# Two attention-and-experts layers on one core: rows asked for ahead of weights, key products of layer two moved, unread products before two waits

## The chip, the cores and the metric

The kernel runs on one core of a Trainium2 chip. The metric is the device time of one launch in microseconds. The engines are TensorE (PE), VectorE (DVE), ScalarE (ACT), GpSimd (POOL) and SyncE (SP), which issues most of the DMAs. They run side by side and wait for each other by semaphores.

## The reference

Four residual steps on `x` of 4 batches x 1024 tokens x 256 values, all in float32:

```python
x = x + attn0(norm(x), ctx, mask)   # 8 heads of 64, 64 context rows of 192 per batch, masked softmax
x = x + ffn0(norm(x))               # 8 experts, top 1, at most 640 rows each: relu(t @ W1) @ W2, W1 256x1024
x = x + attn1(norm(x), ctx)         # 16 heads of 64, no mask
x = x + ffn1(norm(x))               # 8 experts, top 2: silu(t @ W11) * (t @ W12) @ W2, W11 and W12 256x512
```

An expert's rows are picked by the data. In the last step each token goes to its two best experts, and the two results are weighted and added.

## The kernel before, in words

**Attention.** Each layer folds the keys into the query weights and the values into the output weights (`m` and `n`), so that a tile of 128 tokens needs scores (L666), a softmax (ACT L731, POOL L763), a transpose of the probabilities (L638) and the product with `n` (L681). 32 tiles run in a software pipeline: iteration `t` of every engine's list works on tile `t` and, ahead of it or behind it, on others. NT is 32. Every product is made of three matmuls on numbers split in a high part (made by ACT) and a low part (made by DVE): transposed probabilities are split by ACT L712 and DVE L971 before L681 may start. The router's logits (L687) and ranks (L696, L698, L700) are TensorE's too; DVE works out the routing (L806 to L858) in a long row of small steps, one of which (L825) reads exponentials that ACT makes (L725). POOL then scatters each tile's normed rows to their expert in HBM (L752).

**Keys of layer two.** The keys and values of layer two need only the context and weights. They are 16 units (`tensor_kv`, L342), each of two products on 256 columns (four records in the profile), and each is copied out of PSUM by ACT (L350). `KV_AT` gives the units that stand in iterations of layer one's attention, `KV_AFTER` the rest, which come after it. Within an iteration they stand at the end, after the logits; ACT's copies of the same units stand before its softmax and before L725.

**First experts.** SP waits until all scattered rows have landed (`rows_landed`, twelve semaphores), asks for expert 0's rows (`E_xin`, 640 KB), then stores the keys. TensorE finishes `KV_AFTER`, transposes the rows (L1125), ACT and DVE split them (L1192, L1237), and then come 96 matmuls up (L1144) and 120 down (L1161) for each of 8 experts. ACT splits the down weights (L1185) between the last key copy and the rows.

**Second experts.** The routed rows stand in 39 tiles of 256 rows, two tiles in flight (`par`). For tile `i` TensorE makes 48 matmuls up (L1433), four transposes of tile `i+1` (L1406) and 24 matmuls down for tile `i-1` (L1418). A tile's rows (`E_xin`, 260 KB) come with 4 values each, from which DVE makes the row's weight and its place in the output in six small steps (`meta`, `NM` = 6, L1503 to L1508): one after each of four products `E_hf` (L1522), and the last two at the end of the tile (`small.more(NM)`). SP's loop asks for tile `i+1`: the up weights (L1366, 2048 KB), the rows (L1381), the down weights (L1374, 512 KB). A table in SBUF says of each tile whether its expert differs from that two tiles before; where it does not, the weight DMAs are issued but move nothing. The up weights wait until the up products of tile `i-1` are done. The rows wait for all six `meta` steps and for the transposes of tile `i-1`. SP works in order, so what stands behind a waiting instruction waits too. Before each weight DMA SP loads two values from the table.

Of the kernel before, what the change touches and what calls it, by code (L numbers as in the profile page):

```python
# [15 lines left out]
P = 128  # L16
B, SEQ, D = 4, 1024, 256
TOK = B * SEQ
NT = TOK // P
# [21 lines left out]
def is_int(v):  # L41
    return isinstance(v, (int, np.integer))
# [160 lines left out]


ZEROED = 16 * (2 * E + 2)
VECTOR = 2 * E + 1


def attention_setup(p, layer, ins, base, before):
# [3 lines left out]
    PR, W, INNER = H // 2, H * KEYS, H * DH  # L213
# [41 lines left out]
    N_BANK, RING_N = 4, 3  # L255
    UNITS = 2 * PR // 4
    KV_BANKS = (0, 1, 2, 3)
    KV_AT = {NT: range(0, 2), NT + 1: range(2, 5)}
    KV_AFTER = range(5, 2 * PR)

    def kv_ps(j):
        return ps[:, KV_BANKS[j % len(KV_BANKS)], 0:B * KEYS]
# [196 lines left out]
def attention(p, layer, ins, setup, base, before):  # L459
# [8 lines left out]
    PR, W = H // 2, H * KEYS  # L468
# [84 lines left out]
    def cnt(t):  # L553

        return max(0, min(t + 1, NT))
# [64 lines left out]
    def tensor(e, ahead=None):  # L620
        e.wait_ge(p.s_sel, 3)
        for t in iters:
# [33 lines left out]
            if ok(t + 3):  # L656
# [3 lines left out]
                for q in range(NB):  # L660
                    bank = ps[:, S_BANK + ((t + 3) % 2) * NB + q, :]
# [6 lines left out]
                                          stop=(c == KC - 1 and j == 2))  # L668
                mm.then_inc(s_sim, 1)

            need(e, s_res, cnt(t - 1))
            need(e, s_lg, cnt(t - 3))
            if rank_at(t - 1) is not None:
# [10 lines left out]
            if ok(t - 2):  # L684
# [1 line left out]
                for c in range(KC):  # L686
                    mm = e.matmul(ps[:, O_BANK, LOGITS], xfT[:, c, :], wr[:, c, :], start=(c == 0), stop=(c == KC - 1))  # L687
                mm.then_inc(s_lgp, 1)
            if ahead and t in ahead.KV_AT:
                ahead.tensor_kv(e, ahead.KV_AT[t])  # L690
            g = rank_at(t)
            if g is not None:
# [332 lines left out]
def experts_capacity(p, ins, setup, rows_from):  # L1025
# [94 lines left out]
    def transposes(q, e):  # L1120
        q.wait_ge(s_x, 16 * (e + 1))
        wait(q, s_hlo, 2 * FC * e)
        for c in range(TC):
            for kc in range(KC):
                mm = q.transpose(ps[:, X_BANK + c, kc * P:(kc + 1) * P],  # L1125
                                 xin[:, c, kc * P:(kc + 1) * P], p.ident[:, :])
            mm.then_inc(s_xT, 1)

    def tensor(q):
        transposes(q, 0)  # L1130

        def up(e, par, h):
# [169 lines left out]
def experts_top2(p, ins, rows_from):  # L1302
# [3 lines left out]
    NM = 6  # L1306
# [46 lines left out]
    def sync(q):  # L1353
# [7 lines left out]
        def load_up(i, par):  # L1361
            e = expert(i)
            new = None if is_int(i) and i < 2 else changed(i)
            wait(q, s_up, FC * (i - 1))
            land(q, i)
            q.dma_start(up_w[:, par, :, :, :, :].rearrange("p j w c f -> p (j w c f)").bitcast(F32),  # L1366
                        up_d[e, :, :], cond=new).then_inc(s_w[par], 16)
# [24 lines left out]

        def body(i, par, last):
            if not last and not (is_int(i) and i == 0):
                load_up(i + 1, 1 - par)
                load_x(i + 1, 1 - par)
                load_w2(i + 1, 1 - par)
        tiles_loop(q, body)

    def tensor(q):  # L1400
# [41 lines left out]
                down(i, par)  # L1442
        rows_from.need(q, rows_from.s_lg, NT)
        rows_from.need(q, rows_from.s_posr, rows_from.GROUPS)
        transposes(0, 0)
        tiles_loop(q, body)

# [32 lines left out]
    def vector(q):  # L1480
# [36 lines left out]
        def body(i, par, last):  # L1517
            small = meta(i, par)
            for m in range(FC):
                q.wait_ge(s_sg, i * FC + m + 1)  # L1520
                wait(q, s_hlo, (i - 1) * FC + m + 1)
                q.tensor_tensor(hf[:, m, :], ps[:, UP_BANK + m, T1:2 * T1], sg[:, m, :],  # L1522
                                ALU.mult).then_inc(s_hf, 1)
                small.more(1)
                if m == 1:
                    split_w2(i, par)
                if 0 < m < 3:
                    hidden_lo(i, par, m - 1)
            if not last:
                split_x(i + 1, 1 - par)  # L1530
            for m in (2, 3):
                hidden_lo(i, par, m)
            small.more(NM)
            assert small.j == NM
            if not is_int(i) or i > 0:
                outputs(i - 1, 1 - par)
            wait(q, s_mt, NM * (i + 1))
            wait(q, s_add, 16 * TC * (i - 1))
            q.tensor_copy(dest[:, par, :, :], mb[:, :, :])
            if last:  # L1540
                outputs(i, par)
# [122 lines left out]
```

## Time and profile before

| | us |
|---|---|
| median of three timed runs | 1144.49 |
| their lowest and highest | 1144.35, 1146.0 |
| the profiled execution | 1133.49 |
| its span | 1131.7 |

The profiled execution lies 11.0 us under the median of the timed runs. Its time is 1.8 us more than its span. In the profile TensorE is busy for 92% of the span. Layer one's attention ends at about 191 us, the first experts run from 218 to 453, layer two's attention ends at about 746, and the second experts run from 762 to the end. The digits in the row of TensorE's clock are tenths of 2.4 GHz.

### The profile page before, as it was taken

How to read it: one execution, taken by the hardware profiler on the slowest of the kernel's cores; microseconds unless marked ns; L12 is line 12 of the kernel's file. 1: busy time of each engine (PE TensorE's matmuls, PEld its weight loads, DVE VectorE, ACT ScalarE, POOL GpSimd, SP SyncE). 2: the span in 40 equal slices, each digit the busy share in tenths (PEclk: the TensorE clock that was granted, in tenths of full speed). 3: DMA queues.
4: the chain of work that ended last, by engine and by line, in shares of the span. 5: the costliest groups of instructions: out<-in, count | busy, mean ns of one | idle time of the engine just before them, and what ended most of it. 6: DMA issues, size and time to landing. Idle time of an engine off the chain costs nothing.

```text
span 1131.7 us, 25652 instructions
## 1 busy us (share of the span) xinstructions
PE 1044.6 (92%) x7860; PEld 974.0 (86%) x7860; DVE 733.8 (65%) x2273; ACT 672.3 (59%) x2491; POOL 518.5 (46%) x527
## 2 busy tenths in 40 slices
PE   6999997899999999889999999719999999999994
PEld 4688886799999999569999999609999999999994
DVE  6678886344444443867787777646666777766673
ACT  2788885444444443579999999504444444444441
POOL 1346777333333332336588886751333333333333
PEclk9999999799999999999999999958999999999998
DMA  9910002556666657201122221453757755498432
GB/s 323 338 53 25 29 30 80 210 192 226 223 229 229 224 186 234 75 14 39 39 72 71 73 75 57 161 187 117 229 110 201 242 145 158 95 340 252 104 63 29
DMA packets 91045, 163.53 MB, mean 144 GB/s; under 512 B 11858, under 2 KB 70100, under 8 KB 88532
## 3 DMA queue, kind: packets, MB, share of 16 engines
q1 hardware_dynamic: 72868, 134.07, 34.5%
q0 software_dynamic: 17376, 27.15, 11.4%
q10 hardware_dynamic: 720, 1.33, 0.3%
q8 instruction: 39, 0.64, 0.2%
q14 instruction: 42, 0.34, 0.1%
HBM read 159.46 MB, written 63.34 MB: 197 GB/s over the span
## 4 chain that ended last, share of the span: by engine, by line
PE 79%; DVE 8%; DMA 5%; ACT 4%; issue 2%; POOL 1%; SPq 0%; DVEq 0%; ACTq 0%; POOLq 0%
PE psum L1433 15%; PE psum L681 11%; PE psum L666 11%; PE psum L1144 10%; PE psum L1161 10%; PE psum L1418 7%; DMA E_xin<-rows 4%; PE psum L638 4%; PE psum L342 2%; ACT L_prob L731 2%; PE psum L687 2%; PE psum L1406 2%; PE psum L379 1%; DVE L_m_lo L431 1%; PE psum L653 1%
## 5 line engine op out<-in xcount | busy, mean ns | idle before, releaser
L1552 POOL DMA_INDIRECT out<-E_y,E_dest x78 | 121.1, 1553 | 248.0 <-DVE E_y L1514 226.7
L731 ACT ACTIVATE L_prob<-psum,L_neg_max 128x64 f32<-128x64 f32 x768 | 228.6, 362 | 4.8 <-DVE L_neg_max L964 4.7
L1433 PE MATMUL psum<-E_xT_hi,E_up_w 128*128 128x256 f32 x1248 | 225.0, 280 | 2.9 <-DVE E_xT_lo L1493 2.9
L1433 PEld LDWEIGHTS psum<-E_xT_hi,E_up_w 128*128 128x128 f32 x1248 | 194.3, 190 | 3.5 <-DVE E_xT_lo L1493 3.5
L731 ACT ACTIVATION_READ_ACCUMULATOR L_prob<-psum,L_neg_max 128x1 f32 x768 | 195.4, 256 | 0.0
L1433 PE MATMUL psum<-E_xT_lo,E_up_w 128*128 128x256 f32 x624 | 174.6, 280 | 0.0
L1468 ACT ACTIVATE E_sg<-psum 128x256 f32<-128x256 f32 x156 | 59.9, 384 | 172.2 <-PE psum L1433 169.1
L1522 DVE TENSOR_TENSOR E_hf<-psum,E_sg 128x256 f32<-128x256 f32 x156 | 66.0, 423 | 91.6 <-ACT E_sg L1468 91.0
L1433 PEld LDWEIGHTS psum<-E_xT_lo,E_up_w 128*128 128x128 f32 x624 | 118.6, 190 | 0.0
L681 PE MATMUL psum<-L_n_hi,L_pT_hi 128*128 128x256 f32 x384 | 107.9, 281 | 10.9 <-DVE L_pT_lo L971 10.9
L763 POOL TENSOR_TENSOR L_prob<-L_prob,L_rcp 128x512 f32<-128x512 f32 (+1 forms) x64 | 94.3, 1474 | 41.0 <-DVE L_rcp L930 39.5
L1202 ACT ACTIVATE E_h_hi<-psum 128x256 fp32r<-128x256 f32 (+1 forms) x128 | 55.8, 437 | 89.2 <-PE psum L1144 89.2
L681 PE MATMUL psum<-L_n_hi,L_pT_lo 128*128 128x256 f32 x384 | 107.3, 279 | 0.0
L681 PE MATMUL psum<-L_n_lo,L_pT_hi 128*128 128x256 f32 x384 | 107.3, 279 | 0.0
L1245 DVE SCALAR_TENSOR_TENSOR E_h_lo<-psum,E_h_hi 128x256 fp32r<-128x256 f32 (+1 forms) x128 | 62.8, 491 | 55.4 <-ACT E_h_hi L1202 54.6
L1418 PE MATMUL psum<-E_w_hi,E_h_hi 128*128 128x256 f32 x312 | 90.2, 289 | 0.0
L1161 PE MATMUL psum<-E_w_hi,E_h_hi 128*128 128x256 f32 x320 | 90.2, 282 | 0.0
L1161 PE MATMUL psum<-E_w_hi,E_h_lo 128*128 128x256 f32 x320 | 89.6, 280 | 0.0
L1161 PE MATMUL psum<-E_w_lo,E_h_hi 128*128 128x256 f32 x320 | 89.5, 280 | 0.0
L1418 PE MATMUL psum<-E_w_hi,E_h_lo 128*128 128x256 f32 x312 | 87.0, 279 | 0.0
L1418 PE MATMUL psum<-E_w_lo,E_h_hi 128*128 128x256 f32 x312 | 86.9, 279 | 0.0
L681 PEld LDWEIGHTS psum<-L_n_hi,L_pT_hi 128*128 128x128 f32 x384 | 72.9, 190 | 14.9 <-issue 12.3
(198 smaller groups left out, 3089.8 us busy)
## 6 DMA issues: line engine op xcount, KB each, us to landing
E_up_w<-up SPq DMA_DIRECT2D x39, 2048.0 KB
E_w<-in_w SPq DMA_DIRECT2D x39, 512.0 KB
E_w<-in_w SPq DMA_DIRECT2D x16, 1024.0 KB, 7.3
E_xin<-rows SPq DMA_DIRECT2D x39, 260.0 KB, 2.7
E_raw<-in_w SPq DMA_DIRECT2D x16, 512.0 KB, 6.9
up<-E_raw_hi SPq DMA_DIRECT2D x16, 512.0 KB, 6.1
up<-E_raw_lo SPq DMA_DIRECT2D x16, 512.0 KB, 3.7
rows<-zero SPq DMA_DIRECT2D x8, 640.0 KB, 14.5
```

What stands on the lines that cost most here:

```text
L666: mm = e.matmul(bank, a[:, (t + 3) % 2, c, :], m[:, b, c, q * 512:(q + 1) * 512], start=(layer == 1 and c == 0 and j == 0), stop=(c == KC ...
L681: mm = e.matmul(o, a[:, r, :], m[:, b, r, :], start=(r == 0 and j == 0), stop=(r == PR - 1 and j == 2))
L731: last = e.activation(prob[q][:, h * KEYS:(h + 1) * KEYS], scores_ps(t)[:, h * KEYS:(h + 1) * KEYS], ACT.Exp, bias=nmx[:, q, h, :], accum_ ...
L763: e.tensor_tensor(pr, pr, rc[:, q, :, :].to_broadcast([P, H, KEYS]), ALU.mult).then_inc(s_p, 1)
L1144: mm = q.matmul(bank, a[par][:, c, m * P:(m + 1) * P], x[:, c, c0 * P:(c0 + cn) * P], start=(k == 0), stop=(k == 3 * KC - 1))
L1161: mm = q.matmul(bank, a[:, h, m, c * P:(c + 1) * P], w[par][:, m, :], start=(k == 0), stop=(k == 3 * FC - 1))
L1245: q.scalar_tensor_tensor(h_lo[:, h, m, 0:cn * P], ps[:, UP_BANK + m % 4, 0:cn * P], 0.0, h_hi[:, h, m, 0:cn * P].bitcast(F32), ALU.max, AL ...
L1418: mm = q.matmul(ps[:, Y_BANK + c, 0:D], a[:, par, m, c * P:(c + 1) * P], w[:, par, m, :], start=(k == 0), stop=(k == 3 * FC - 1))
L1433: mm = q.matmul(bank, up_w[:, par, half, w, c, m * P:(m + 1) * P], x[:, c, :], start=(k == 0), stop=(k == 3 * KC - 1))
L1468: q.activation(sg[:, m, :], ps[:, UP_BANK + m, 0:T1], ACT.Silu).then_inc(s_sg, 1)
L1522: q.tensor_tensor(hf[:, m, :], ps[:, UP_BANK + m, T1:2 * T1], sg[:, m, :], ALU.mult).then_inc(s_hf, 1)
L1552: q.indirect_dma_start(p.out[:, :], bass.IndirectOffsetOnAxis(ap=dest[:, par, c, :], axis=0), y[:, par, c, :], None, compute_op=ALU.add).t ...
```

## The change

Five edits. (1) In the second experts' SP loop the rows of tile `i+1` are asked for before its up weights. (2) DVE makes two `meta` steps after each of the first three `E_hf`, and none at the tile's end. (3) Six key units move into iterations NT-2 and NT-1, ahead of that iteration's wait for the split probabilities; two stand in NT and one in NT+1 (before: two and three), and seven after the attention (before: eleven). (4) and (5): before the transposes of the first experts and of the second experts TensorE waits for `rows_landed` and then makes six products of the identity with itself that nobody reads.

```diff
+def keep_busy(q, p, bank):
+    for j in range(6):
+        q.matmul(p.psum[:, bank, 0:P], p.ident[:, :], p.ident[:, :], start=True, stop=True)
...
-    KV_AT = {NT: range(0, 2), NT + 1: range(2, 5)}
-    KV_AFTER = range(5, 2 * PR)
+    KV_AT = {NT - 2: range(0, 3), NT - 1: range(3, 6), NT: range(6, 8), NT + 1: range(8, 9)}
+    KV_AFTER = range(9, 2 * PR)
...
+            if ahead and t < NT and t in ahead.KV_AT:
+                ahead.tensor_kv(e, ahead.KV_AT[t])
             need(e, s_res, cnt(t - 1))
...
-            if ahead and t in ahead.KV_AT:
+            if ahead and t >= NT and t in ahead.KV_AT:
                 ahead.tensor_kv(e, ahead.KV_AT[t])
...
     def tensor(q):
+        rows_from.rows_landed(q)
+        keep_busy(q, p, 5)
         transposes(q, 0)
...
             if not last and not (is_int(i) and i == 0):
+                load_x(i + 1, 1 - par)
                 load_up(i + 1, 1 - par)
-                load_x(i + 1, 1 - par)
                 load_w2(i + 1, 1 - par)
...
         rows_from.need(q, rows_from.s_posr, rows_from.GROUPS)
+        rows_from.rows_landed(q)
+        keep_busy(q, p, Y_BANK)
         transposes(0, 0)
...
-                small.more(1)
+                small.more(NM // 3)
...
-            small.more(NM)
             assert small.j == NM
```

TensorE's list in layer one's attention, iteration NT-2, before: the logits of the iteration before it (`wr`), the transposes of the probabilities (`L_prob_70`) and of the normed rows (`L_stage`), and the first product with `n`:

```order
L687 MATMUL psum<-wr,L_xfT 128x8 x2
L638 MATMUL psum<-ident,L_prob_70 128x128 x4
L653 MATMUL psum<-ident,L_stage 128x128 x2
L681 MATMUL psum<-L_n_hi,L_pT_hi 128x256
L681 MATMUL psum<-L_n_hi,L_pT_lo 128x256
L681 MATMUL psum<-L_n_lo,L_pT_hi 128x256
```

The same place now (lines are numbered anew by the change: L645, L660 and L690 are the old L638, L653 and L681, L349 the old L342):

```order
L696 MATMUL psum<-wr,L_xfT 128x8 x2
L645 MATMUL psum<-ident,L_prob_70 128x128 x4
L660 MATMUL psum<-ident,L_stage 128x128 x2
L349 MATMUL psum<-L_ctxT,L_wk 128x256 x6
L690 MATMUL psum<-L_n_hi,L_pT_hi 128x256
L690 MATMUL psum<-L_n_hi,L_pT_lo 128x256
L690 MATMUL psum<-L_n_lo,L_pT_hi 128x256
```

Six products, two for each of three key units, stand ahead of the product with `n`; iteration NT-1 has the same.

SP's list in the second half of the second experts' loop, before. `E_up_w` are the up weights, `E_xin` the rows, `tab` the table:

```order
L1359 TENSOR_LOAD tab
L1359 ISA x2
L1366 ISA
L1366 DMA E_up_w<-up 128x4096
L1377 ISA
L1377 TENSOR_LOAD tab
L1377 ISA x2
L47 REGISTER_ALU
L1381 ISA
L1381 DMA E_xin<-rows 128x2x260
```

The same place now (L1388 and L1392 are the old L1377 and L1381, L1366, L1370 and L1377 the old L1355, L1359 and L1366):

```order
L1388 ISA x2
L47 REGISTER_ALU
L1392 ISA
L1392 DMA E_xin<-rows 128x2x260
L1366 ISA
L1366 TENSOR_LOAD tab
L1366 ISA x2
L1370 ISA
L1370 TENSOR_LOAD tab
L1370 ISA x2
L1377 ISA
L1377 DMA E_up_w<-up 128x4096
```

Both table loads of the up weights (L1366, L1370) now stand between the DMA of the rows and that of the weights; before, they stood ahead of the weights' wait.

DVE's list in the same loop, before, from a tile's last `E_hf` on; `E_xT_lo` is the next tile's split, `E_mb` the last `meta` steps:

```order
L1522 TENSOR_TENSOR E_hf<-psum,E_sg 128x256
L47 REGISTER_ALU
L1506 SCALAR_TENSOR_TENSOR E_mb<-E_xin,shift 128x2
L1493 TENSOR_TENSOR E_xT_lo<-psum,E_xT_hi 128x512
L1483 TENSOR_TENSOR E_h_lo<-E_hf,E_h_hi 128x256 x2
L47 REGISTER_ALU
L1507 TENSOR_TENSOR E_mb<-E_mb,spare 128x2
L47 REGISTER_ALU
L1508 TENSOR_TENSOR E_mb<-E_mb,E_xin 128x2
```

And now, from the tile's third `E_hf` on (L1535, L1506, L1496, L1520, L1521 are the old L1522, L1493, L1483, L1507, L1508):

```order
L1535 TENSOR_TENSOR E_hf<-psum,E_sg 128x256
L47 REGISTER_ALU
L1520 TENSOR_TENSOR E_mb<-E_mb,spare 128x2
L47 REGISTER_ALU
L1521 TENSOR_TENSOR E_mb<-E_mb,E_xin 128x2
L1496 TENSOR_TENSOR E_h_lo<-E_hf,E_h_hi 128x256
L1533 REGISTER_ALU
L1535 TENSOR_TENSOR E_hf<-psum,E_sg 128x256
L1506 TENSOR_TENSOR E_xT_lo<-psum,E_xT_hi 128x512
L1496 TENSOR_TENSOR E_h_lo<-E_hf,E_h_hi 128x256 x2
```

The last two `meta` steps stood behind the last `E_hf`, the split and two `E_h_lo`; now they stand ahead of all of them.

## Rows read from the trace of the kernel before

**Rows 1.** The page: busy time, TensorE's and the clock's tenths in 40 slices.
```profile
PE 1044.6 (92%) x7860; PEld 974.0 (86%) x7860; DVE 733.8 (65%) x2273; ACT 672.3 (59%) x2491; POOL 518.5 (46%) x527
PEclk9999999799999999999999999958999999999998
```

**Rows 2.** Chain of waits, second experts, longest pieces: start us, us, what.
```profile
881.81 6.76 DMA E_xin<-rows
...
888.61 0.66 PE psum L1406 x4
...
892.01 5.44 PE psum L1433 x48
897.45 0.44 PE psum L1406 x4
```

**Rows 3.** Waits from 730 to 1131 us: engine line <- releaser: us, times, longest.
```profile
PE psum L1406 <- DMA E_xin<-rows: 21.7, 8, 15.9
PEld psum L1406 <- DMA E_xin<-rows: 7.4, 8, 1.4
```

**Rows 4.** Timeline of SP, second experts: start us, us, what.
```profile
879.17 0.36 SPq L1366 DMA_DIRECT2D E_up_w<-up  x1
881.81 0.38 SPq L1381 DMA_DIRECT2D E_xin<-rows  x1
883.67 0.37 SPq L1374 DMA_DIRECT2D E_w<-in_w  x1
...
986.11 0.35 SPq L1366 DMA_DIRECT2D E_up_w<-up  x1
```

**Rows 5.** Timeline of DVE, 872 to 893 us: start us, us, what.
```profile
878.62 0.42 DVE L1522 TENSOR_TENSOR E_hf<-psum,E_sg 128x256 f32<-128x256 f32 x1
...
881.39 0.16 DVE L1508 TENSOR_TENSOR E_mb<-E_mb,E_xin 128x2 f32<-128x2 f32 x1
```

**Rows 6.** Windows: us, busy PE, PEld, DVE, ACT, POOL, PEclk, DMA share, GB/s.
```profile
880.00:886.00 6.00, 6.00 (x55) 6.00 (x54) 3.87 (x13) 2.52 (x6) 2.84 (x2) 1.00 0.96 353
987.00:1024.00 37.00, 35.06 (x303) 34.42 (x302) 24.85 (x75) 16.78 (x40) 12.44 (x8) 1.00 1.02 337
```

**Rows 7.** Timeline of PE, 172 to 222 us: with idle before and its releaser.
```profile
184.38 0.36 PE L681 MATMUL psum<-L_n_hi,L_pT_hi 128*128 128x256 f32 x1 [1.29 <-DVE L_pT_lo L971]
...
218.37 0.69 PE L1144 MATMUL psum<-E_xT_hi,E_w_hi 128*128 128x384 f32 x1 [2.54 <-DVE E_xT_lo L1237]
```

**Rows 8.** Timeline of ACT, 176 to 222 us.
```profile
210.63 0.38 ACT L350 ACTIVATE L_kv<-psum 128x256 f32<-128x256 f32 x1 [0.48 <-PE psum L342]
...
214.36 1.90 ACT L1185 ACTIVATE E_w_hi<-E_w 128x2048 fp32r<-128x2048 f32 x1
216.17 1.47 ACT L1192 ACTIVATE E_xT_hi<-psum 128x256 fp32r<-128x256 f32 x5
```

**Rows 9.** Timeline of DVE, 185 to 222 us.
```profile
201.72 0.17 DVE L825 TENSOR_REDUCE L_r<-L_ex 128x2 f32<-128x16 f32 x1 [2.61 <-ACT L_ex L725]
216.57 1.75 DVE L1237 TENSOR_TENSOR E_xT_lo<-psum,E_xT_hi 128x256 fp32r<-128x256 f32 x5 [5.34 <-ACT E_xT_hi L1192]
```

**Rows 10.** Line L1074 on SP, 200 to 215 us: issue, and us to landing.
```profile
L1074 SPq DMA_DIRECT2D E_xin<-rows x1: 367/367/367, 208.7 to 208.7; - x1
DMA to landing us min/median/max: 5.1/5.1/5.1
```

**Rows 11.** Windows around the two starts of the experts, columns as in Rows 6.
```profile
217.60:224.40 6.80, 6.03 (x19) 6.03 (x20) 1.83 (x5) 1.02 (x3) 3.30 (x1) 0.50 0.86 290
764.30:770.60 6.30, 6.21 (x29) 6.21 (x30) 0.79 (x4) 2.56 (x5) 0.00 (x0) 0.50 0.79 309
```

**Rows 12.** Chain of waits, start of the second experts.
```profile
758.92 2.77 DMA E_xin<-rows
...
761.83 1.10 PE psum L1406 x4
...
764.39 8.71 PE psum L1433 x48
```

## The prediction

> **What bounds the kernel now.** I read the page first: TensorE is busy for 92% of the span and its clock is at full level but for a dip where the second experts start [rows 1]. So time is to be had only where TensorE idles or runs at the lower clock. Next the chain of waits, which shows TensorE almost everywhere and, in the second experts, pieces of 6 to 7 us of "DMA E_xin<-rows" in seven places, of which one is shown [rows 2]. Such a piece is not its price: the transfer runs beside TensorE's work. The price is in the waits. TensorE waited 21.7 us for these rows, 15.9 of them before the first tile, so 5.8 us in seven places. Its weight loads give 7.4 us in eight places, none over 1.4 [rows 3]. The first transposes after such a wait also take 0.66 us where others take 0.44 [rows 2], and 5.8 + 7 x 0.22 = 7.3 us. I take 7.4 us as what the seven waits cost, about 1.06 each.
>
> Why the rows are late stands in SP's timeline. The up weights (2048 KB) are asked for at 879.17, the rows at 881.81, and the rows land 6.76 us after that [rows 2, 4]. SP sat between the two for `meta`, whose last step started at 881.39 [rows 5]. From 880 to 886 us the DMA engines moved 353 GB/s x 6.00 = 2118 KB [rows 6], about the weights (2048 KB are 2097 thousand bytes), and only after that the rows came.
>
> **The change: rows ahead of weights, and `meta` earlier.** The third `E_hf` started at 878.62 [rows 5]. One chained step more stands before it now, some 0.2 us, it takes 0.3 until the next may start, and two steps of 0.2 follow, so the last starts near 879.35 and not at 881.39. SP's DMA stood 0.42 behind it (881.39 to 881.81), so the rows are asked for near 879.8, with no 2 MB ahead of them. TensorE wants them at 888.61 less the wait of up to 1.4, at 887.2. That is 7.4 us for a transfer of 260 KB that took 2.77 us alone [rows 12]. All seven waits go, -7.4 us.
>
> What is late next are the up weights. They now stand behind the rows' wait, the rows' DMA and their own two table loads. From the rows' DMA to the down weights', with two table loads between, SP took 883.67 - 881.81 = 1.86 us [rows 4]. So the up weights are asked for at 879.8 + 1.86 = 881.7, 2.5 us later than before. If their bytes take as long (879.17 to 886.0 is 6.8 us), they land at 888.5. The up products would start at 892.01 - 1.4 = 890.6. The margin is 2.1 us, and no wait follows. The down weights are asked for 1.86 us later still, at 883.5, where they were (883.67). The tightest place is where four sets of weights follow each other. An issue of up weights that moves bytes takes about 0.36 us on SP, one that moves none 0.08; of the first kind the loop has fourteen, and four of them start tile after tile from 986.11 on [rows 4]. From 987 to 1024 us the DMA engines are full without a break (share 1.02) [rows 6], four sets in 37 us or 9.25 each, against a tile's pitch of 897.45 - 888.61 = 8.8. Each set falls back by 0.4 to 0.5, the fourth by about 2, which uses up the margin. I count 0.6 us lost there. DVE does the same steps, three of them earlier, beside waits for ACT. The second experts give -7.4 + 0.6 = **-6.8 us**. Bounds: -7.4, and above nothing if the weights come later than I reckon (a rival below).
>
> **Key units.** A unit takes 0.86 us at the full clock (0.48 + 0.38 between the starts of two copies) [rows 8]. In NT-2 and NT-1 TensorE idled 1.29 us before the product with `n`, waiting for DVE's split [rows 7]; three units take 2.6, so each of the two iterations is longer by 1.3 and the attention's end comes 2.6 us later. That is paid back in NT+1, where one unit stands for three: before, DVE sat 2.61 us at L825, whose exponentials ACT made only after its key copies [rows 9]. Now that wait goes. DVE's last routing steps, POOL's last scatters and SP's DMA for the first expert's rows (208.7 us) stay within 0.3 us of where they were. They land 5.1 us after it [rows 10], at 213.8.
>
> What moves is TensorE and ACT between the two. After the attention seven units stand and not eleven. The seventh copy started at 210.63 [rows 8], so ACT's split of the down weights (1.90 us from 214.36) now ends near 212.9, before the rows land, where it held up ACT's split of the rows until 216.17 [rows 8]. Now: rows at 213.8, the first pair of transposes 0.25, ACT's first of five pieces 0.3 (1.47 / 5) [rows 8], DVE's five 1.75 [rows 9], and the up products start near 216.2. With the clock at its lower level the ten transposes take 10 x 0.27 (four took 1.10 us at that level [rows 12]), and the start is 213.8 + 2.7 + 0.3 + 0.35 = 217.2. Before: 218.37 [rows 7]. The gain is 2.2 or 1.2; since TensorE now idles about 2 us before the rows, I take **-1.5 us**. Bounds: the clock's lower level lasted 6.8 us from there [rows 11], at a loss of half of it, 3.4 us. A phase of the clock that falls otherwise moves this by up to 1.7 either way, so from +0.5 to -3.5.
>
> **Unread products.** No row shows a float32 product of 128 columns that isn't a transpose. By the unit of keys (two products of 256 columns in 0.86 us) six take 1.3 us at full clock, 2.6 at half. Before the second experts they start no later than SP's DMA behind the same waits, 758.92, and end by 761.5, before the rows are in at 761.69 [rows 12]: hidden, with up to 0.4 us lost if a semaphore comes late. Before the first experts they run from about 211 to 213. Do they raise the clock? Before the second experts, TensorE was 6.21 of 6.30 us busy at 0.50, and before that the first up products 6.03 of 6.80 [rows 11]. A burst of 2.6 us and one of 1.1, with gaps of at least 0.3 and of 1.5, is less than what failed to raise it for 6 us there. I take 0, with bounds +0.4 and -7.3 (next part).
>
> **Sum.** -6.8 - 1.5 + 0 = -8.3 us. The profiled execution has 1133.49 (span 1131.7, 1.8 around it) and would have 1125.2. The timed runs' median is 1144.49, 11.0 above it, in a way that the profile doesn't show. I take the same difference for it: 1136.2.
>
> **Rivals.** (A) The clock rises early. The products that start at 764.39 took 8.71 us, a later tile's 5.44 [rows 2, 12], and the transposes 1.10 for 0.44: 3.9 us. With the 3.4 of the first experts 7.3 us more go: 1128.9. For it: only the lower level stands there. Against it: rows 11. Chance 0.10. The Trainium skill, "TensorE: Matmul & The Clock Gate", section "Part 1: The HAM clock gate", says that the throttled state is the default and that activity releases it; by that rule these unread products would bring such a gain, and the trace agrees only as far as work without gaps goes.
>
> (B) The keys bring nothing. If DVE's 2.61 us do not come back (another wait takes its place, as ACT's copies in NT-1 do to its exponentials), the rows land 2.6 us later, the first up products start near 218.9, and 0.5 us is lost instead of 1.5 won: 1138.2. For it: DVE's steps follow one upon another there. Chance 0.17.
>
> (C) The 11 us between timed and profiled execution are slower transfers. Then more than 7.4 us go with the waits. With half of the 11 in these places: 1130.7. Nothing in the profile shows it. Chance 0.08.
>
> (D) The change doesn't do what it says: the rows stay late in the sets that follow upon each other, since the previous down weights stand ahead of them in the queue. Then the three waits of that stretch and the weights' own lateness leave half of the 7.4: 1139.9. Against it: these are only 512 KB. Chance 0.05.
>
> (E) Slower: the up weights are late. They are asked for 2.5 us later in each of fourteen loads that move bytes. From ask to need there are 890.6 - 881.7 = 8.9 us. Once a load takes longer, each further 0.1 us costs up to 1.4 us in all, and from 9.5 us (14 x 0.6 = 8.4) the change loses. At 9.9 us it costs 14.0 for the 0.6 counted: -8.3 - 0.6 + 14.0 = +5.1, 1149.6. For it: a set in full traffic takes 9.25 us. Against it: that holds the down weights and the scattered results too, and the up weights come first but for the rows. Chance 0.08.
>
> **How the numbers follow.** The forecast has 0.52; its own range is 1134 to 1138.5. The range 1130.5 to 1141 holds it with B, C and D, and leaves out A and E, 0.18. About 0.2% (2.3 us) is what the measurement tells from no change. Faster: the forecast, A, B, C and most of D, less a small rest for sums that fail together: 0.85. Same 0.07, slower 0.08.
>
> **What would show it.** In the profile after: no wait of TensorE for `E_xin` behind the first tile; SP's DMA of the rows near 0.4 us behind the last `meta` step, that of the up weights 1.9 behind it; no wait of L1433's line for a DMA, except up to 0.6 us in the stretch of four sets. The attention of layer one ends 2.6 us later and the scatters don't. The first up products start at 216 to 217.4. The second experts' first 48 products take 8.7 us still. I am wrong if TensorE waits for `E_up_w` in more than two tiles, if the rows' DMA before the first experts moves by over 1 us, or if the clock row is higher at either start.

## The result, and the profile after

| | forecast | measured |
|---|---|---|
| median of the timed runs, us | 1136.2 (1130.5 to 1141) | **1127.0** (1123.5 to 1132.3, six runs) |
| the kernel before, beside it | | 1143.3 (1137.7 to 1146.0, six runs) |
| ratio to before | 0.993 | 0.9865, interval 0.983 to 0.9901 |
| profiled execution and span | 1125.2 | 1130.32, 1128.6 |

The change is faster, as forecast, but by 15.4 us (1143.3 x 0.0135) instead of 8.3, and the time lies below the range. In this document two kinds of number have to be kept apart. The two profiled executions lie only 3.2 us apart (1133.49 and 1130.32), the medians of the timed runs 16.3 us. So the gain must not be read from these two profiles alone.

The page after, the rows that answer to [rows 1]:

```profile
PE 1052.6 (93%) x7884; PEld 981.6 (87%) x7884; DVE 736.1 (65%) x2273; ACT 675.2 (60%) x2491; POOL 523.5 (46%) x527
PEclk9999999899999999889999999868999999999997
```

TensorE is busy 8 us longer, for the same products and twelve unread ones, of which 1.60 and 2.90 us are seen in its timeline. The rest goes with its clock: at the lower level a product takes longer, the clock's row has five slices of 8 where it had two, and the mean granted clock of the span is 0.964 where it was 0.972.

The steps of the second experts, against [rows 3 to 5]. DVE's third `E_hf` with the last `meta` steps behind it, then SP (start us, us, what), then TensorE's waits from 785 us on (us, times, longest), then TensorE's timeline of the same tile:

```profile
879.34 0.42 DVE L1535 TENSOR_TENSOR E_hf<-psum,E_sg 128x256 f32<-128x256 f32 x1
879.67 0.15 DVE L1520 TENSOR_TENSOR E_mb<-E_mb,spare 128x2 f32<-128x2 f32 x1
879.86 0.16 DVE L1521 TENSOR_TENSOR E_mb<-E_mb,E_xin 128x2 f32<-128x2 f32 x1
```

```profile
880.28 0.38 SPq L1392 DMA_DIRECT2D E_xin<-rows  x1
882.36 0.36 SPq L1377 DMA_DIRECT2D E_up_w<-up  x1
```

```profile
PE psum L1444 <- DMA E_up_w<-up: 1.0, 3, 0.4
```

```profile
879.11 0.60 PE L1417 MATMUL psum<-ident,E_xin 128*128 128x128 f32 x4
...
887.73 0.60 PE L1417 MATMUL psum<-ident,E_xin 128*128 128x128 f32 x4
891.43 0.38 PE L1444 MATMUL psum<-E_xT_hi,E_up_w 128*128 128x256 f32 x1 [0.36 <-DMA E_up_w<-up]
```

The rows are asked for 0.42 us behind the last `meta` step, and no wait for `E_xin` is left (the transposes of 887.73 have no idle time in brackets). Now the weights come last, in three tiles, for 1.0 us in all. The chain of waits has the piece that the forecast had reckoned with 6.8 us (an estimate from bytes; no row of the trace before has the landing of the weights):

```profile
882.36 8.95 DMA E_up_w<-up
```

The start of the first experts, against [rows 7, 8]: the chain of waits, and TensorE's timeline.

```profile
208.12 2.37 DMA rows<-L_stage,row
...
218.65 15.80 PE psum L1155 x96
```

```profile
213.33 1.60 PE L211 MATMUL psum<-ident 128*128 128x128 f32 x12 [0.47 <-ACT L_kv L357]
215.96 1.31 PE L1134 MATMUL psum<-ident,E_xin 128*128 128x128 f32 x10 [1.02 <-DMA E_xin<-rows]
```

The twelve records of L211 are the six unread products. The ten transposes behind them take 1.31 us, so the clock is at its full level there. Two windows tell of the clock (columns as in [rows 6]):

```profile
218.60:222.10 3.50, 3.45 (x11) 3.45 (x12) 0.56 (x1) 0.49 (x1) 1.09 (x1) 0.51 1.00 413
```

```profile
762.50:768.80 6.30, 4.02 (x17) 3.36 (x17) 0.69 (x1) 1.44 (x2) 0.00 (x0) 0.50 0.88 279
```

At the first start half level (0.51, which is 1.2 GHz) lasted 3.4 us, where it was 6.8 before [rows 11]. At the second start it went on, in spite of the six unread products, until 771.6 us.

All three signs that the prediction named for being wrong are there: TensorE waits for `E_up_w` in three tiles and not in two at most, SP asks for the first experts' rows at 210.82 us and not at 208.7, and the clock's row has an 8 at the first start where it had a 7. The experiments tell which of them matter.

### The profile page after: what moved, and what is told of

Same layout as the page of the kernel before. It is cut to its first block, busy times and chain, and to the rows that moved or that the text cites. A ratio compares the mean times of both kernels' runs of the same rounds, so it can differ in the third digit from the quotient of the medians.

```text
span 1128.6 us, 25710 instructions
## 1 busy us (share of the span) xinstructions
PE 1052.6 (93%) x7884; PEld 981.6 (87%) x7884; DVE 736.1 (65%) x2273; ACT 675.2 (60%) x2491; POOL 523.5 (46%) x527
## 4 chain that ended last, share of the span: by engine, by line
PE 81%; DVE 6%; DMA 4%; issue 3%; ACT 3%; POOL 1%; SPq 1%; DVEq 0%; ACTq 0%; POOLq 0%
PE psum L1444 17%; PE psum L690 12%; PE psum L673 11%; PE psum L1155 10%; PE psum L1172 10%; PE psum L1429 8%; PE psum L645 3%; DMA E_up_w<-up 2%; PE psum L386 2%; ACT L_prob L740 2%; PE psum L696 2%; PE psum L1417 1%; PE psum L660 1%; DVE L_m_lo L438 1%; PE psum L349 1%
## 5 line engine op out<-in xcount | busy, mean ns | idle before, releaser
L1564 POOL DMA_INDIRECT out<-E_y,E_dest x78 | 126.2, 1618 | 234.8 <-DVE E_y L1527 110.8
L690 PE MATMUL psum<-L_n_hi,L_pT_hi 128*128 128x256 f32 x384 | 109.0, 284 | 8.3 <-DVE L_pT_lo L980 8.3
L690 PE MATMUL psum<-L_n_lo,L_pT_hi 128*128 128x256 f32 x384 | 108.1, 282 | 0.0
L690 PE MATMUL psum<-L_n_hi,L_pT_lo 128*128 128x256 f32 x384 | 108.1, 282 | 0.0
L1535 DVE TENSOR_TENSOR E_hf<-psum,E_sg 128x256 f32<-128x256 f32 x156 | 65.7, 421 | 55.7 <-ACT E_sg L1481 54.9
L673 PE MATMUL psum<-L_m_hi,L_xT_hi 128*128 128x512 f32 x192 | 82.9, 432 | 2.0 <-ACT L_prob L740 2.0
```

What stands on the lines that cost most here:

```text
L673: mm = e.matmul(bank, a[:, (t + 3) % 2, c, :], m[:, b, c, q * 512:(q + 1) * 512], start=(layer == 1 and c == 0 and j == 0), stop=(c == KC ...
L690: mm = e.matmul(o, a[:, r, :], m[:, b, r, :], start=(r == 0 and j == 0), stop=(r == PR - 1 and j == 2))
L1564: q.indirect_dma_start(p.out[:, :], bass.IndirectOffsetOnAxis(ap=dest[:, par, c, :], axis=0), y[:, par, c, :], None, compute_op=ALU.add).t ...
```

## The experiments

"Ratio" is to the kernel before on the same chip, with its 95% interval. "Start to end" is from the second experts' first up product to the end of the span. It needs a profile and leaves out what happened earlier. Of each kernel I also read where the clock went to half level around the first experts' start. Most kernels here have one profile, so differences between profiles alone can be chance; the timed runs decide.

**How far the profile of before stands for the kernel.** No edit.

> The kernel before, unchanged, once more. Its profiled execution (span 1131.7 us) lay 10 us under its timed runs, and the change gained 15.4 us in the timed medians but only 3.1 us between the two profiles. Theory N (noise of the clock): what differs from execution to execution is where TensorE's clock falls to its lower level in the two attentions, and the second experts take 367 us from the first up product to the end in every execution of this kernel. Then this profile shows that stretch within 1.5 us of 367.3, and the rest longer by what the row of the granted clock shows. Theory T (transfers): the waits for E_xin in the second experts are longer in the slower executions. Then the stretch is 375 to 380 us and TensorE waits for E_xin 12 to 18 us there, not 5.8. Timed: within 0.3% of before in both.

Ratio 1.0007 (0.9981 to 1.0032), median 1142.35 of 12 runs (1136.7 to 1149.1), span 1138.8. The same kernel took 7.1 us longer in its second profile. Stage by stage from the span's start: 0.7 at the end of the first experts, 2.9 in attention two, 1.6 between SP's first ask for rows and the second experts' first up product (5.5 and 7.1 us), 1.9 from there to the end (367.3 and 369.2). TensorE's waits for the rows behind the first tile were not 5.8 us but:

```profile
PE psum L1406 <- DMA E_xin<-rows: 6.8, 9, 1.7
```

In attention two the two profiles differ in the stretches of 3 to 7 us at half clock: before had none between 489 and 508 us, this one has two, 494.8 to 498.2 and 505.0 to 508.4. The timed runs say the same: over the 32 of the kernel before on this chip, time and mean granted clock have a correlation of -0.77, and their mean clock is 0.965, where the profiled execution of before had 0.972. So the 11 us between profile and median were in the main a short profile with a high clock. For slower transfers (rival C) there is 1.0 us of waits in 7.1: it has nearly nothing to stand on.

**The parts alone, and the whole once more.**

```diff
# rows_first: edits 1 and 2
+                load_x(i + 1, 1 - par)
                 load_up(i + 1, 1 - par)
-                load_x(i + 1, 1 - par)
...
-                small.more(1)
+                small.more(NM // 3)
...
-            small.more(NM)
# keys_moved: edit 3
+    KV_AT = {NT - 2: range(0, 3), NT - 1: range(3, 6), NT: range(6, 8), NT + 1: range(8, 9)}
+    KV_AFTER = range(9, 2 * PR)
...
# unread: edits 4 and 5
+        rows_from.rows_landed(q)
+        keep_busy(q, p, 5)
...
+        rows_from.rows_landed(q)
+        keep_busy(q, p, Y_BANK)
```

> Edits 1 and 2 alone (rows asked for ahead of the up weights, two meta steps after each of the first three products); keys and unread products as before. Theory N: the second experts give the 7.5 us that lie between the two profiles there (367.3 against 359.8), so -7 us (0.994) and the other half of the 15.4 us comes from the other edits. Theory T: -12 to -16 us (0.987 to 0.990), nearly the whole.

> Edit 3 alone (six key units into NT-2 and NT-1, seven after the attention). By the prediction -1.5 us at most; by the profile after, where the first up products started at 218.65 us against 218.37, nothing. Theory N: the clock falls less often at the end of layer one's attention when TensorE is given work in NT-2 and NT-1, and -3 to -6 us come of it in the mean. Theory T: 0 to -1.5 us.

> Edits 4 and 5 alone (six unread products before the transposes of the first and of the second experts). The prediction: nothing. Theory N allows a part here: if the burst makes the clock rise one step earlier in a share of the executions, -1 to -3 us in the mean. Theory T: within 1 us.

> The changed kernel once more, on the same chip as the next three. So far: 0.9865 for it, and 0.9931, 0.9984 and 0.9975 for its parts alone, product 0.9890. Theory P (the parts add up): 0.988 to 0.990, -12 to -13 us. Theory I (keys and unread products help each other, or the rows first need one of them): 0.985 to 0.987, -15 to -17 us. The stretch from the first up product of the second experts to the end is 360 to 365 us, against 367 to 373 in kernels that ask for weights first.

| kernel | ratio | median, us | start to end, us |
|---|---|---|---|
| rows_first | 0.9931 (0.9907 to 0.9954) | 1135.56 | 365.1 |
| keys_moved | 0.9984 (0.9964 to 1.0004) | 1141.89 | 373.2 |
| unread | 0.9975 (0.9952 to 0.9998) | 1137.98 | 365.4 |
| full | 0.9868 (0.9817 to 0.9919) | 1126.37 | 364.7 |

The rows ahead of the weights give 7.9 us (1142.1 x 0.0069), more than the 6.8 forecast. The keys give 1.8, in an interval that holds 0. The unread products, forecast at 0, give 2.9 (1142.1 x 0.0025), just clear of nothing. The whole once more gives 15.1 us, as in the result. What is left of the waits for the up weights in rows_first:

```profile
PE psum L1433 <- DMA E_up_w<-up: 2.4, 3, 1.9
```

**Which burst it is.** Edit 4 alone, edit 5 alone, and the changed kernel without both.

```diff
# no_unread, against the changed kernel
     def tensor(q):
-        rows_from.rows_landed(q)
-        keep_busy(q, p, 5)
         transposes(q, 0)
...
-        rows_from.rows_landed(q)
-        keep_busy(q, p, Y_BANK)
         transposes(0, 0)
```

> Only the six unread products before the first experts, the rest as before. The two together gave 0.9975. If the gain is at the first experts, where TensorE had idled for less than 3 us and its clock stood at the full level until 217.6: 0.9975, -3 us. If at the second: 1.000. The prediction's step (a burst shorter than what failed to raise the clock raises nothing) gives 1.000 for both.

> Only the six unread products before the second experts, where the clock is at the lower level for 20 us before. If the gain is here, the clock rises 3.4 us earlier in a share of the executions, worth 1.7 us each: at most 0.9985, -1.7 us. Else 1.000.

> The changed kernel without both unread bursts: rows first and keys moved. Theory P: 0.9915, -9.6 us. If the bursts are worth more once the keys are moved (TensorE idles before the first experts' rows only then), full is more than 3 us faster than this one, with this one at 0.9915 still.

| kernel | ratio | median, us |
|---|---|---|
| unread_first | 0.9952 (0.9919 to 0.9985) | 1136.33 |
| unread_second | 0.9983 (0.9954 to 1.0013) | 1137.38 |
| no_unread | 0.9895 (0.9851 to 0.9939) | 1128.33 |

This points at the first burst. Alone it gives 5.5 us by the ratio, the second 1.9, which can't be told from nothing; their intervals overlap. Whether the parts add up is not settled: 0.9931 x 0.9984 x 0.9952 = 0.9868 is what full measured, but with the two bursts as measured together (0.9975) the product is 0.9890, and the intervals allow both.

**Do edits 1 and 2 work apart?**

```diff
# order_only: the first two lines of rows_first; meta_only: the other three
```

> Edit 1 alone: the rows are asked for ahead of the up weights, but the last two meta steps still stand at the tile's end. The rows' request then waits for meta (near 881.5 in the tile of the trace before) and the up weights 1.86 us longer, so near 883.7, 4.5 us later than before. By the prediction's sum (6.8 us from request to landing, 890.6 wanted) the weights come at 890.5 alone and at 892 to 893 in the second of a pair and where four follow each other: rows_first's gain of 7.9 us shrinks by 14 loads x 0.5 to 1, to 1.000 to 0.994. Theory of the rival (late weights decide): slower than before, 1.003 or more. If meta does not matter: 0.9931 as rows_first.

> Edit 2 alone: two meta steps after each of three products, the up weights still asked for first. The rows' request moves 2 us forward but stays behind 2 MB in the queue, so they land only when the weights have: 0 to -2 us, 0.998 to 1.000, and TensorE's waits for E_xin stay at 5 to 10 us. If it was SP's wait for meta and not the queue that made the rows late, 0.993.

order_only 1.0067 (1.0022 to 1.0113), median 1149.83: slower, as the rival's theory had it and not as the prediction's sum (0.994 to 1.000). Its twelve runs fall in two groups, four from 1137.8 to 1140.5 us and eight from 1147.3 to 1156.0, and the profiled one (1140.31) is of the shorter group. Even so its start to end is 376.8 us, longer than in any other kernel. meta_only 1.0015 (0.9979 to 1.0051), 1144.26: no gain. TensorE's waits behind the first tile, order_only and meta_only:

```profile
PE psum L1433 <- DMA E_up_w<-up: 12.7, 8, 2.3
```

```profile
PE psum L1406 <- DMA E_xin<-rows: 10.7, 9, 1.8
```

With the order alone, the rows still wait for the late `meta` steps, and now the 2 MB of weights wait behind them. In order_only TensorE's timeline and SP's show how late:

```profile
876.91 0.60 PE L1406 MATMUL psum<-ident,E_xin 128*128 128x128 f32 x4
...
890.84 0.38 PE L1433 MATMUL psum<-E_xT_hi,E_up_w 128*128 128x256 f32 x1 [1.57 <-DMA E_up_w<-up]
```

```profile
880.06 0.38 SPq L1381 DMA_DIRECT2D E_xin<-rows  x1
882.14 0.36 SPq L1366 DMA_DIRECT2D E_up_w<-up  x1
```

The weights are asked for 5.2 us behind the start of the transposes (882.14 - 876.91). In the changed kernel it is 3.25 (882.36 - 879.11). Of these 2 us 1.2 come back as the longer wait, 1.57 against 0.36. `meta` alone, on the other hand, brings the rows' DMA forward but leaves 2 MB ahead of it in the queue, and the waits stay.

**The first burst alone beside the other edits, and the second start tried harder.**

```diff
# both_more, against the changed kernel
...
-    for j in range(6):
+    for j in range(n):
...
+                known = expert(i + 1), changed(i + 1)
                 load_x(i + 1, 1 - par)
-                load_up(i + 1, 1 - par)
-                load_w2(i + 1, 1 - par)
+                load_up(i + 1, 1 - par, known)
+                load_w2(i + 1, 1 - par, known)
...
+        keep_busy(q, p, Y_BANK, 34)
         rows_from.rows_landed(q)
-        keep_busy(q, p, Y_BANK)
+        keep_busy(q, p, Y_BANK, 10)
```

`known` makes SP load the table's two values once, ahead of the rows' wait. first_burst_only is the changed kernel without edit 5.

> The changed kernel without the unread burst before the second experts. Theory F (what the prediction missed is that the burst before the first experts keeps the clock from falling while TensorE idles there: 6 of 6 profiles without it have 7 us at the lower level around the first up products, the four with it 0, 0, 0 and 3.4): as full, 0.987, the clock row at 0 or 3.4 us of the lower level there. If the second burst carries it: as no_unread, 0.9895.

> The changed kernel with two additions: SP loads the two table values of a tile before it waits for meta (the up weights go out 0.4 us behind the rows, not 2.1), and the burst before the second experts is 34 unread products before rows_landed and 10 after. Expected: TensorE's waits for E_up_w go from 1.4 us (mean of four profiles) to 0, the clock is at its full level when the second experts' first rows land, the first 48 up products take 5.5 to 5.9 us and not 7.2 to 8.7, and the transposes 0.5 and not 1.1. Together -3 to -5 us on full: 0.983. If the clock falls again between the bursts, -1.5 us.

first_burst_only 0.9856 (0.9803 to 0.9909), 1124.16; both_more 0.9855 (0.9799 to 0.9912), 1124.27. The second burst adds nothing that can be seen (full, with it: 0.9868), and both_more missed its forecast of 0.983 though its steps came out nearly as forecast. In both_more SP's spacing from the rows to the up weights is 0.74 us and no longer 2.08:

```profile
1000.80 0.37 SPq L1390 DMA_DIRECT2D E_xin<-rows  x1
1001.54 0.34 SPq L1376 DMA_DIRECT2D E_up_w<-up  x1
```

The wait for the up weights shrank to 0.3 us. And 34 + 10 products did raise the clock at the second start. TensorE's timeline there:

```profile
748.06 10.45 PE L211 MATMUL psum<-ident 128*128 128x128 f32 x68 [1.42 <-DVE L_ranks L950]
760.92 2.47 PE L211 MATMUL psum<-ident 128*128 128x128 f32 x20 [2.42 <-DMA rows<-x,L_row]
...
765.77 0.38 PE L1443 MATMUL psum<-E_xT_hi,E_up_w 128*128 128x256 f32 x1 [1.48 <-DVE E_xT_lo L1506]
772.97 0.66 PE L1416 MATMUL psum<-ident,E_xin 128*128 128x128 f32 x4 [1.28 <-DMA E_xin<-rows]
```

```profile
765.00:772.00 7.00, 5.92 (x48) 5.71 (x48) 4.02 (x13) 4.21 (x8) 0.00 (x0) 1.00 0.89 355
```

The clock is at 1.00 where it was 0.50, and the 48 products are through 1.3 us before the next tile's rows: these stand behind tile 1's 2.5 MB in the queue (8.14 us in the chain of waits). Part of what the clock gives becomes a wait for a transfer.

**The first burst once more, on other edits, and all together.**

```diff
# all_more, against both_more
         q.dma_start(xin[:, 0, :, :], ...)
-        q.wait_ge(rows_from.s_tab, 2)
-        load_up(1, 1)
-        load_w2(1, 1)
         rows_from.tails_landed(q)
         q.wait_ge(rows_from.s_tab, 3)
         load_x(1, 1)
+        load_up(1, 1)
+        load_w2(1, 1)
```

no_burst_again is the kernel of no_unread, first_burst_again that of first_burst_only. keys_and_first has edits 3 and 4.

> The changed kernel without both unread bursts, a second time: 0.9895 as before (-12 us); its profile has 7 us of the lower clock around the first experts' first up products (212 to 219 us in the first profile of it).

> The changed kernel with the first burst alone, a second time. Theory F (the burst before the first experts is the term that the forecast set to 0): 3 to 4 us faster than no_burst_again, 0.986. Theory G (it is noise, and the bursts are worth nothing): within 1.5 us of no_burst_again.

> The keys moved and the burst before the first experts, weights asked for first and meta as before. If the parts add up: 0.9984 x 0.9965 = 0.995, -6 us. If keys and burst gain more together than apart, 0.992 or less, since the full change less the rows' part is 0.9865 / 0.9931 = 0.9934. If they need the rows-first edits: 0.997 or more.

> both_more (table values loaded before the wait for meta, 34 unread products before rows_landed and 10 after, before the second experts), and tile 1's rows asked for ahead of tile 1's weights too. In both_more the first 48 up products ran at the full clock, but tile 1's rows came 8.1 us after their request, behind 2.5 MB, and its transposes started only at 772.97, 7.2 us after the first up product. Expected: they come 3 us after the request, the second tile's up products start 7.5 us after the first's and not 9.3, so -2 us on both_more: 0.983 to 0.984. If tile 1's up weights are now late, nothing.

| kernel | ratio | median, us |
|---|---|---|
| no_burst_again | 0.9899 (0.9857 to 0.9941) | 1128.67 |
| first_burst_again | 0.9865 (0.9816 to 0.9914) | 1124.46 |
| keys_and_first | 0.994 (0.9913 to 0.9968) | 1133.58 |
| all_more | **0.9824** (0.9784 to 0.9864) | **1121.32** |

no_burst_again and first_burst_again ran beside each other on one chip. Twice the same pair: 1128.3 to 1124.2 (in different rounds; 4.4 us by the ratios), and 1128.7 to 1124.5 (3.9). The first burst is worth some 4.2 us on top of the other edits. The intervals of the ratios overlap. Of the runs themselves all six of first_burst_only (1121.4 to 1125.8) lie under all six of no_unread (1125.9 to 1129.9), and five of the six of first_burst_again under all six of no_burst_again. keys_and_first, 0.994, is what keys and burst give if they add up. The window behind the first rows' landing, no_burst_again and first_burst_again:

```profile
206.40:213.00 6.60, 3.92 (x19) 3.11 (x17) 2.29 (x1) 3.71 (x6) 0.38 (x1) 1.00 0.51 166
213.00:220.00 7.00, 5.85 (x21) 5.48 (x22) 2.68 (x6) 2.40 (x6) 4.15 (x1) 0.51 1.02 417
```

```profile
206.20:213.00 6.80, 5.71 (x32) 4.70 (x32) 2.29 (x1) 3.72 (x6) 0.57 (x1) 1.00 0.55 188
213.00:220.00 7.00, 5.62 (x36) 5.38 (x36) 3.40 (x8) 2.99 (x9) 3.99 (x1) 1.00 1.00 413
```

TensorE's timeline at the first rows, and the chain of waits with the first 96 up products, no_burst_again:

```profile
213.22 2.37 PE L1134 MATMUL psum<-ident,E_xin 128*128 128x128 f32 x10 [2.90 <-DMA E_xin<-rows]
```

```profile
216.52 15.79 PE psum L1153 x96
```

And first_burst_again:

```profile
210.59 1.60 PE L211 MATMUL psum<-ident 128*128 128x128 f32 x12 [0.47 <-ACT L_kv L357]
212.82 1.31 PE L1134 MATMUL psum<-ident,E_xin 128*128 128x128 f32 x10 [0.62 <-DMA E_xin<-rows]
```

```profile
215.51 14.24 PE psum L1155 x96
```

Until the rows come the clock is at 1.00 in both. Without the burst TensorE sits idle for 2.90 us, and the clock falls for the 7 us in which the transposes and first up products run. With the burst the idle time is cut in a 0.47 and a 0.62, behind the transposes stands one of 1.38, and the clock stays up. All nine profiles of kernels without the first burst have such a low stretch of about 7 us at this start. Of the nine with it, seven have none, and two (the changed kernel's and all_more's) have one of 3.4 us. The 96 up products take 14.2 us in those seven, 15.8 to 17.0 in the other eleven. Where TensorE idles depends on the keys. With eleven units behind the attention it waits 2.54 us behind the transposes, as in [rows 7] (five profiles); with seven it waits 2.74 to 2.90 ahead of them (three); order_only, whose rows came early, has 1.66 ahead of them. In all nine profiles with the burst the longest idle stretch there is 1.38 us, and the two that still have 3.4 us of half clock are those with the longest gap ahead of the transposes, 1.02 and 1.06 us (the other seven: up to 0.84).

all_more is the fastest version: 20 us under before by its ratio, and 3.1 us under first_burst_again beside it, with intervals that overlap. Its wait for `E_xin` and `E_up_w` behind the first tile is gone altogether, and its start to end is 354.0 us, against a mean of 362.7 in the four kernels with edits 1 and 2 (rows_first, changed, full, no_unread). Compared with both_more, too, the gain of 3 us lies within the intervals.

## Why the prediction was wrong in size and right in sign

Both in the timed median (1127.0 against 1136.2) and in the gain (15.4 against 8.3) the forecast is too small. Of the 7.1 us of gain that it lacks, 3.4 are the unread products, for which it had put 0 (15.4 - 12.0, no_unread), 1.4 are rows and keys, each alone over its forecast (1.1 and 0.3), and 2.3 are what rows and keys gave together over the two alone (12.0 - 9.7). Only the first of these is a step that was wrong in kind.

**Rows ahead of weights: right.** Forecast -6.8, alone -7.9, and by the profiles 369.1 - 362.7 = 6.4 us (mean of six profiles with the weights first, and of the four with the rows first). The mechanism was as told: 0.42 us from the last `meta` step to the rows' DMA, then no wait for rows. Two numbers in it were off and cancelled out, which is luck. The seven waits [rows 3] were those of the short profile. The mean over six is 9.4 us by the weight loads, in eight to eleven places. And the margin of the up weights was not 2.1 us. They took 8.95 us from ask to landing and not 6.8. Rows and scattered results run beside them, but what share of the 2.15 us is theirs no run tells. The weights' ask stands 2.08 us behind the rows' (forecast 1.86). Of the 9.4 us some 1.4 came back as waits for the weights. By -7.4 + 0.6 the forecast had a small loss on a small gain.

**Rival D** (rows late behind the previous set) has its mechanism in part and no price. In full the rows of the tiles behind tile 1 took up to 6.2 us from ask to landing where sets follow each other and 2.7 elsewhere, and TensorE waited for none of them.

**Rival E has its mechanism, not its size.** order_only is the case in which the weights are late: 12.7 us of waits, 1.0067. The changed kernel stands at that edge: in three tiles its weights are late by up to 0.4 us. What keeps it from going over is edit 2. Here SP's two table loads are a part: 2.08 us with both between the DMAs, 0.74 with none, so 0.67 each. The Trainium skill, "DMA: Bandwidth & Descriptors", section "Latency and other measured facts", gives a `tensor_load` a floor of about 600 ns. The trace of the changed kernel agrees only for a load together with the instructions around it: the two records of the load there last 0.27 and 0.28 us, and they start 0.66 us apart (880.80 and 881.46).

**Keys: as forecast, with no proof by time.** -1.5 forecast, -1.8 measured, in an interval that holds 0. That the two agree is no evidence by itself. The profiles carry it better. From SP's ask for the first rows to the first up product it took 9.7 to 11.1 us in seven of the eight profiles with the keys where they were (before: 9.7, [rows 7, 10]; order_only: 8.5), and 7.8 to 8.6 in the ten with the keys moved. The forecast was 8.5 with the clock low (217.2 - 208.7) and 7.5 with it high: it was 8.4 to 8.6 in the three without the first burst, 7.8 to 8.1 in the seven with it. Rival B would have the ask itself 2.6 us later. It stands at 207.1 to 210.8 us with the keys moved and at 206.2 to 211.7 without, on the mean no later. From the last product with `n` to the ask it took 18.7 us in both profiles of before, and 16.1 to 16.5 in nine of the ten with the keys moved (18.2 in keys_moved itself): what the two longer iterations cost came back there. B falls.

**Unread products: the step that failed.** The prediction said "I take 0", because two bursts are "less than what failed to raise it for 6 us there". That reasoned about raising a clock that is down. It mostly holds for the second start: the clock had been low for some 20 us before the burst (from 740.9 in the changed kernel), and six products changed nothing in three of four profiles. The first 48 up products took 7.2 to 8.6 us in the three kernels with both bursts, and 7.2 to 8.7 in those with none there: where in that range depends on when the low stretch happens to end. The fourth, unread_second, is an exception: there the clock was up from 769.7 us, ahead of the first up product, and they took 5.9 us; but it fell again for 3.4 us at 779.9, and the ratio shows no gain. Whether the burst did that, one profile can't tell.

But at the first start the clock was not down. The window 206.4 to 213.0 of no_burst_again shows it at 1.00. It fell where TensorE idled for 1.7 to 2.9 us close to the rows' landing, and it did so with the keys where they were too: unread_first, the burst alone, gives 5.5 us without any key moved. I had read the clock's row as full but for the second experts, though it has a 7 at 198 to 226 us [rows 1]; I had even written down 2 us of idle time, and taken the half clock behind them as given [rows 11]. What was to be asked was whether the burst would *keep* the clock. It does in seven profiles of nine, and in part in two.

By rows: ten transposes took 1.31 us for 2.37, and the 96 up products 14.24 for 15.79, 2.6 us in sum. From SP's ask for the rows to the end of these products 2.3 of them are left (22.15 for 24.41). The medians give 4.2. Beside the rest stands less half clock elsewhere: the mean granted clock of the six runs is 0.974 and 0.973 with the burst, 0.966 and 0.967 without, by my estimate 15 us less at half level (0.0068 x 1126 x 2), of which only 6.8 lie at the first start. In the profiles attention two has 3.4 and 6.8 us of it with the burst and 17.1 without, but the changed kernel and both_more have the burst and 17.1 too. Whether the burst brings this about is not shown.

The Trainium skill, "TensorE: Matmul & The Clock Gate", section "Part 1: The HAM clock gate", has both directions: activity lifts the throttle, and an idle stretch brings it back. In the prediction I weighed it only for the first. The trace agrees with both: in both_more the clock rose at 753.6 us, 5.5 us into the unread products that start at 748.06, and in no_burst_again it fell at the end of the 2.90 us of idle time.

**Rival A** said that the clock would rise early at both starts, for 7.3 us. It had the first start right in effect, with another mechanism (the clock does not fall), and the second wrong.

**The sum.** Without the bursts the forecast was -8.3, and no_unread measured -12 (1141 x 0.0105), no_burst_again the same. rows_first and keys_moved alone give -9.7. With intervals of 2 to 5 us to either side this difference is not settled. One candidate shows in the profiles: attention two has low-clock stretches of 3 to 7 us at places that differ from kernel to kernel and from execution to execution of the same kernel, so a part that shifts the start of attention two may gain or lose there. I have not tested that. It would need many profiles of the same kernel.

## What to carry to other kernels

Where TensorE is about to idle for 2 or 3 us with its clock up, just ahead of a long stretch of products, a handful of unread products in that gap may be worth more than it looks: some 4.2 us here, 2.3 of them seen at the place itself, for 1.6 us of work nobody waits for. Where the clock is already low, the same handful gave nothing that could be measured, and a long burst helps only if the transfers behind the start are early enough too. If you bring one transfer forward, reckon the time to landing of what is now behind it from a row with both in flight, and check what makes the first one wait: here the order without the earlier `meta` steps is a loss of 0.7%, and with them a gain of 0.7%.

## What the runs showed of the hardware

- Two executions of one kernel differed by 7.1 us of span. One profile may be far from the median, and a forecast's terms need the waits of more than one.
- The gap of 2.90 us was followed by 6.8 us at 1.2 GHz though the clock was at 2.4 GHz up to the gap; with idle stretches of 0.47, 0.62 and 1.38 us, and products between them, there was no such stretch.
- A load of a value from a table in SBUF costs SP 0.67 us with the checks and register instructions that go with it; its own record is 0.27 us. In the second experts an issue of a DMA that moves nothing takes SP 0.07 to 0.09 us, and one that moves 0.33 to 0.39.
- The up weights (2 MB) behind a small transfer of rows took 8.95 us to land in the changed kernel; where TensorE waited for them in the other kernels with rows first it was 8.8 to 10.7 us.
